# Cross-attention on one core: where the rest tiles' sum joins GpSimd's sum of the softmax weights

## What is computed

```python
q = (hidden_state @ Wq + bq).reshape(b, l, KVH, GROUPS, HD).transpose(0, 2, 3, 1, 4)
k = (encoder_hidden_state @ Wk + bk).reshape(b, s, KVH, HD).transpose(0, 2, 1, 3)
v = (encoder_hidden_state @ Wv + bv).reshape(b, s, KVH, HD).transpose(0, 2, 1, 3)
scores = jnp.einsum('bkgld,bksd->bkgls', q, k) * scale
scores = scores + encoder_attention_mask[:, :, None, :, :]
attn = jax.nn.softmax(scores, axis=-1)
out = jnp.einsum('bkgls,bksd->bkgld', attn, v)
out = out.transpose(0, 3, 1, 2, 4).reshape(b, l, H)
x = (out @ Wo + bo) + hidden_state
return (x - mu) * jax.lax.rsqrt(var + EPS) * gamma + beta
```

## Time and profile before

| | |
|---|---|
| Median of 3 runs | 3806.91 us (3805.49 to 3808.13) |
| Profiled execution, its own time | 3810.74 us |
| Its span, first to last instruction | 3809.1 us |
| Mean granted TensorE clock | 0.987 of full speed |
| Busy shares of the span: PE, DVE, ACT, POOL | 98%, 66%, 52%, 76% |
| Attention stage, about | 700 to 3450 us |

### The profile page before, as it was taken

One profiled execution on the slowest core, in us unless ns is written; L12 is line 12 of the kernel. 1 busy time (PEld: TensorE's weight loads), 2 busy tenths in 40 slices (PEclk: granted clock), 3 DMA queues, 4 the chain that ended last, 5 costly groups with the idle time before them and its releaser, 6 DMA issues. The chain is left out here.

```text
span 3809.1 us, 54629 instructions
## 1 busy us (share of the span) xinstructions
PE 3745.5 (98%) x20306; PEld 2391.2 (63%) x20306; DVE 2530.3 (66%) x2918; ACT 1992.8 (52%) x3865; POOL 2886.0 (76%) x1104
## 2 busy tenths in 40 slices
PE   8999999989999999999999999999999999999998
PEld 7999877755555555555555555555555555547886
DVE  3334555377777777777777777777777777736675
ACT  2222122126666667667667667667666666661110
POOL 1111111139999999999999999999999999994654
PEclk9999999969999999999999999999999999999999
DMA  5335677527777767777677677777667767777763
GB/s 178 138 139 182 213 255 254 168 64 155 151 147 155 151 147 155 151 148 156 148 148 156 149 149 156 149 147 157 149 146 158 150 143 160 155 169 215 202 190 124
DMA packets 297548, 612.08 MB, mean 161 GB/s; under 512 B 132064, under 2 KB 169056, under 8 KB 264800
## 3 DMA queue, kind: packets, MB, share of 16 engines
q0 software_dynamic: 58080, 337.15, 39.4%
q1 hardware_dynamic: 235968, 265.54, 25.9%
q10 hardware_dynamic: 3264, 6.29, 0.5%
HBM read 244.50 MB, written 96.99 MB: 90 GB/s over the span
## 5 line engine op out<-in xcount | busy, mean ns | idle before, releaser
L1028 DVE TENSOR_REDUCE half_max<-score 128x1 f32<-128x800 f32 (+1 forms) x2048 | 1923.2, 987 | 655.0 <-PE score L883 646.0
L803 POOL TENSOR_TENSOR sum_pool<-sum_pool,weights 128x2048 f32<-128x2048 f32 x446 | 2141.7, 4802 | 32.2 <-ACT weights L1087 4.7
L1087 ACT ACTIVATE weights<-logit 128x512 f32<-128x512 f32 (+1 forms) x3328 | 1700.0, 613 | 707.4 <-PE logit L928 657.2
L928 PE MATMUL logit<-qk_store 98*128 98x512 f32 (+1 forms) x3328 | 1186.2, 424 | 5.2 <-DMA qk_store<-parts_t 3.1
L883 PE MATMUL score<-qk_store 96*128 96x400 f32 (+1 forms) x4096 | 1150.4, 368 | 11.8 <-issue 9.1
L883 PEld LDWEIGHTS score<-qk_store 96*128 96x128 f32 x4096 | 720.1, 192 | 390.1 <-DVE half_max L1028 198.4
L928 PEld LDWEIGHTS logit<-qk_store 98*128 98x128 f32 (+1 forms) x3328 | 608.0, 185 | 399.7 <-ACT weights L1087 261.1
L938 PE MATMUL mixed<-weights,v_sb 128*32 128x512 f32 x6656 | 822.0, 601 | 0.0
L938 PEld LDWEIGHTS mixed<-weights,v_sb 128*32 128x32 f32 x6656 | 170.8, 109 | 361.6 <-issue 285.1
L803 POOL TENSOR_TENSOR sum_pool<-weights 128x2048 f32<-128x2048 f32 x64 | 294.8, 4606 | 62.2 <-ACT weights L1087 59.6
L514 POOL DMA_DIRECT2D q_parts<-o_hi x64 | 34.5, 540 | 310.8 <-DMA q_parts<-o_lo 220.8
(11 more groups left out here) (84 smaller groups left out, 2700.2 us busy)
## 6 DMA issues: line engine op xcount, KB each, us to landing
weights<-weights POOLq DMA_DIRECT2D x191, 1024.0 KB, 7.9
sum_pool<-weights POOLq DMA_DIRECT2D x63, 1024.0 KB, 7.0
qk_store<-q_parts SPq DMA_DIRECT2D x192, 256.0 KB, 4.0
qk_store<-k_parts SPq DMA_DIRECT2D x192, 200.1 KB, 6.9
rows<-in_ctx SPq DMA_DIRECT2D x26, 1024.0 KB, 5.2
landing<-in_mask_Bx1xSxS_ff SPq DMA_DIRECT2D x32, 800.5 KB, 7.1
rows<-in_x SPq DMA_DIRECT2D x16, 1024.0 KB, 6.4
q_parts<-o_hi POOLq DMA_DIRECT2D x64, 256.0 KB, 2.4
```

What stands on the lines that cost most here:

```text
L803: nc.gpsimd.tensor_tensor(sum_pool[s % 2][0:w], first[0:w], weights[buffer(s, st)][0:w], ALU.add).then_inc(pool_added, 1)
L928: last = nc.tensor.matmul(bank[0:w, :], k_sb[s][:, keys], q_sb[s][:, h, :], start=True, stop=not masked, skip_group_check=masked)
L1028: nc.vector.tensor_reduce(half_max[m // NROW % 2][:, k % G, k // G, j:j + 1], score[j][:, :, 0:HALVES[j][2]], mybir.AxisListType.XY, ALU.m ...
L1087: nc.scalar.activation(weights[buffer(s, st)][0:w, h, :], logit[u % BANKS][0:w, :], ACT.Exp).then_inc(exp_done, 1)
```

## The change

The merge is no longer a transfer. VectorE does it with one `tensor_tensor` add of 128x2048 elements, ahead of its reduction 10 of a step (`MERGE_K` = 10, where TensorE has its first three mixes in a row; in the very first step there is none). It waits for the third rest transfer and for the eighth GpSimd add of the step before. `rest_merged` now counts by 1 and is waited for by number of steps. GpSimd's first rest transfer of a step (k = 1) waits in addition until the merge of the step before is done.

```diff
-    MERGE_AT = 1
+    MERGE_K = 10
...
                 if k == 1:
                     pool.wait_ge(mix_done, quad * (QUAD * ST) + (s * ST + REST[0] + 1 + MIX0))
+                    if step:
+                        pool.wait_ge(rest_merged, step)
...
-            def merge(step, s):
-
-                pool.wait_ge(pool_added, step * NPOOL + NPOOL)
-                pool.wait_ge(rest_added, step * (16 * (len(REST) - 1)) + 16 * (len(REST) - 1))
-                pool.sem_inc(pool_seen, 1)
-                pool.dma_start(sum_pool[s % 2][:], weights[buffer(s % QUAD, REST[0])][:], accum_op=ALU.add).then_inc(rest_merged, 16)
...
                     add(quad, s, n)
-                    if n == MERGE_AT and not first:
-                        merge(quad * QUAD + (s - 1), s - 1)
...
-                pe.wait_ge(rest_merged, step * 16 + 16)
+                pe.wait_ge(rest_merged, step + 1)
...
+            def merge(step, s):
+
+                dve.wait_ge(rest_added, step * (16 * (len(REST) - 1)) + 16 * (len(REST) - 1))
+                dve.wait_ge(pool_added, step * NPOOL + NPOOL)
+                nc.vector.tensor_tensor(sum_pool[s % 2][:], sum_pool[s % 2][:], weights[buffer(s % QUAD, REST[0])][:], ALU.add).then_inc(rest_merged, 1)
...
                             copy_lo(quad * QUAD + (s + 1))
+                        if k == MERGE_K + 2 * (LEAD - lead) and not (first and s == 0):
+                            merge(quad * QUAD + (s - 1), s - 1)
                         if s == 2 and k == 8 and not first:
                             invert(quad - 1)
...
-                        act.wait_ge(rest_merged, quad * (16 * QUAD) + (16 * before + 16))
+                        act.wait_ge(rest_merged, quad * QUAD + (before + 1))
```

## The result

The changed kernel takes 3949.22 us (median of 4 runs, 3946.53 to 3949.98), the kernel before 3807.52 us in the runs beside it: a ratio of 1.0371 (95% interval 1.0353 to 1.0389), +141.7 us. The forecast was 3884 with a range of 3842 to 3975. The range holds it; the forecast case does not, and the first rival's "lost and won rounds alternate", 3947, comes nearest.

The account below looks back on a forecast made before the run. TensorE was taken to bound the attention step at 40.67 us, GpSimd's chain 0.17 us behind. From the 3806.91 us median, +56 us for the port and 8 x 2.6 us for lost rounds (+77) gave 3884 us, range 3842 to 3975.

Parts of the forecast that it names:

- forecast case: Attention steps: the merge mostly starts before GpSimd's second add (a won round); +50 to +115 us, chance 0.53.
- lost and won rounds alternate: Attention steps: the merge misses the gap before GpSimd's second add every other step; +140 us, 3947; rival 1, 0.27 in all.
- The port: VectorE's two-SBUF-input merge and GpSimd's adds exclude each other; GpSimd's chain grows 1.11 to 41.61 us, the step 0.94.
- x - 1.06: TensorE's stall before the thirteenth score when GpSimd trails by x us; settles at x = 2.0 with 0.94 us a step.
- The wait on VectorE: The merge waits for the previous step's third rest transfer; missing the gap at x = 0 stalls TensorE 3.55 us.
- The number of lost rounds: Steps where the merge starts after GpSimd's second add: three at start-up, three or four relapses, 8 in all.
- From x = 2 on nearly all make it: With GpSimd trailing 2 us, nearly all third rest transfers land before the gap; the 12.4 us one just misses 12.2.
- What a lost round costs: A step whose merge misses the gap is 2.6 us dearer net than a step at 0.94; 8 x 2.6.
- Rival 2: GpSimd is hardly held by VectorE's merge; step cost 0.3 to 0.7 us, +20 to +45, 3827 to 3852 us; chance 0.12.
- All lost: The merge misses the gap in every attention step: 3.55 x 62 = +220 us, 4027; chance 0.08 within rival 1's 0.27.
- No change: VectorE's merge and GpSimd's adds run side by side, the merge hides in 2.50 us of idle time; 3807 us, chance 0.05.
- faster: No lock, and the row maxima's small transfer lands in time, so TensorE's waits go: 15 us back, 3792 us; chance 0.03.

Follow-up runs that it names:

- e1: Changed kernel with VectorE's add left out and its two waits kept; 3805.51 us, ratio 0.9998.
- e5: Changed kernel with SyncE's query and key loads after the third rest transfer's landing, and the row maxima's transfer ahead of the denominators' store; 3862.15 us, ratio 1.0136.
- e2: Changed kernel with VectorE's add replaced by a maximum over the same 128x2048 elements, one SBUF input; 3809.89 us, ratio 1.0005.
- e3: Changed kernel with SyncE's loads of queries and keys sent only after the third rest transfer has landed; 3910.31 us, ratio 1.028.
- e8: As e5, but the merge waits for GpSimd's second add of the step, so it always misses the gap; 4149.68 us, ratio 1.0899.
- e7: Kernel before, its merging transfer kept, plus an independent two-input VectorE add of 128x2048 at the merge's place; 4003.57 us, ratio 1.0516.
- e4: Changed kernel with the row maxima's transfer put ahead of the denominators' store in SyncE's queue; 3973.97 us, ratio 1.0418.

## Why the prediction was right, and where it was wrong

- *Who sets the step.* Right. TensorE sets 40.67 us with GpSimd 0.17 behind. Taking the merge's issue away alone (e1) gains nothing, as a bound on TensorE demands; adding 0.94 us to GpSimd's chain costs 0.94.
- *The port.* Right, and the size too. n=1 takes 6.46 us, the won step 41.63 for 41.61, and e5 gives +56.3 for +56. e2 against the changed kernel isolates it, with the output-stage rows beside it. The row of 4.37 us in the output stage was enough to see the hold and its size before. One slip is harmless: by the rows of the prediction TensorE stalls for x - 1.16 (2019.06 less 2016.85 + 1.05), not x - 1.06, so GpSimd trails by 2.1 and the sum changes by 0.1 us.
- *The wait on VectorE.* Right that it decides whether a round is won, and that SyncE's loads slow the landing (e3: 7.0 us without them). By itself it costs nothing (e1).
- *The number of lost rounds.* Wrong: 16 for 8. The step that failed is "From x = 2 on nearly all make it". Issue and gap both follow GpSimd's own timing, so x cancels and the window stays at 10.2 us, where I had 12.2. What trailing does change is that the loads are nearer their end: in the middle they began 1.6 us ahead of the third issue before, and 3.6 in trailing rounds. With it the middle landing falls from 11.2 to 9.8 us. That wins most rounds, and leaves one in five late.
- *What a lost round costs.* Mis-sized: 4.4 us above a won step, for 2.6. The stall was right at x = 0 (3.40 to 3.65 us for 3.55). The clock behind it, 1.3 to 2.2 us, was missing, and so was what trailing adds: the 7 rounds lost while trailing make steps of 46.4 us in the mean, the other 9 of 45.7. 16 x 4.4 = 70.5, and 13.5 for the four steps with a wait for the row maxima, where I had 8 x 2.6 = 21. The difference of 63 us is nearly the whole distance from 3884 to 3949.
- *The rivals.* The range held the result because it took in "alternate", not because the forecast case (+50 to +115) was right. "Alternate" hit 3947 by luck, with another make-up: 0.26 of the rounds lost and 0.94 a step from the port, not half of them lost. Rival 2 is out, a won step costs the full 0.94. "All lost" was priced at +220; e8 measures +342. "No change" and "faster" are out: only with GpSimd's add taken away does the merge cost nothing.
- *The small transfer of the row maxima.* I looked at it only as a source of gain, and put it at nothing in the sum. It became a loss of 13.5 us in four steps, and the round behind each of them is lost; see below.

## What to carry to other kernels

An idle stretch on VectorE is not free room while GpSimd works back to back. Look at the operands first: a VectorE operation with two SBUF inputs and a GpSimd one run one after the other, and the price lands on whichever of them has less slack (here 0.17 us a step), while a VectorE reduction of the same length cost nothing. The number of tiles read is not the whole of it. In the output stage of the kernel before, a `tensor_scalar` that reads one SBUF tile and two numbers per partition takes 0.81 us with no GpSimd add beside it, and 2.17 beside one; it ends 0.55 us after that add:

```profile
3555.06 0.81 DVE L1321 TENSOR_SCALAR total<-total,moments,spread 128x1024 f32<-128x1024 f32 x1
...
3532.34 2.17 DVE L1321 TENSOR_SCALAR total<-total,moments,spread 128x1024 f32<-128x1024 f32 x1
...
3531.57 2.39 POOL L1371 TENSOR_TENSOR total<-total,beta_row 128x1024 f32<-128x1024 f32 x1
```

No run here goes into that form, so look for a row of the very form that you want to move. Where such an operation must fit a gap between two others, ask how late each of its waits can come, measured from the engine that opens the gap, and what a miss costs in full, with the wait of the bounding engine and the time at the lower clock behind it.

## What the runs showed that I had not expected

**The clock falls behind TensorE's longer waits.** Before, TensorE's clock stays at its upper level from 860 to 3385 us. In the changed kernel 20 low stretches, 116 us in all, lie there, each behind a wait; e8 has 55 of them, 287 us. In e5 TensorE waits too, but briefly, and there is none. Its waits, 1000 to 3200 us (total, times, longest):

```profile
PE score L879 <- DVE half_max L1024: 44.9, 53, 0.9
```

So 0.9 us at a time for 53 times brought none. In the changed kernel all 20 low stretches stand behind waits of 2.04 us or more, and none of its 25 waits of 0.3 to 1.80 us has one behind it. The length of the wait alone does not tell, though: in e7 a wait of 1.16 us at 2530.9 us has a low stretch of 6.8 us behind it, and five waits of 2.73 to 2.76 us have none. What else decides stays open.

**A large transfer from GpSimd's queue holds a small one.** Where GpSimd trails, its second rest transfer is under way when the 8 KB of row maxima should land. In the changed kernel their transfers take 1.8 us in the middle where no rest transfer is under way (22 of 128), and 3.5 where one is. No run takes the rest transfer away, so the hold is read from this comparison. And TensorE's first logits wait for them in half of the steps. Changed kernel, SyncE's queue, then TensorE, then GpSimd's next first add:

```profile
2134.28 2.49 SPq L689 DMA_DIRECT2D qk_store<-parts_t  x2
```

```profile
2140.80 1.22 PE L921 MATMUL logit<-qk_store 98*128 98x512 f32 x2 [2.12 <-DMA qk_store<-parts_t]
```

```profile
2150.79 4.59 POOL L803 TENSOR_TENSOR sum_pool<-weights 128x2048 f32<-128x2048 f32 x1 [3.92 <-ACT weights L1088]
```

The windows that follow that wait:

```profile
2141.00:2144.00 3.00, 3.00 (x10) 1.82 (x14) 1.28 (x2) 1.09 (x2) 3.00 (x3) 0.50 1.07 286
```

TensorE waits 2.12 us, works on at the lower level, everything behind it is late, and GpSimd idles 3.92 us. VectorE's last reduction before the merge then ends 5.00 us after n=0's start, and the round is lost although the transfer it needs landed long before. What makes it late is its place in SyncE's queue: it stands behind the denominators' store, which waits for TensorE. Moving it ahead took away all of these waits (e4, e5), and paid only together with the loads' move.
